# Moving two transposes to other PSUM banks and small steps from VectorE to GpSimd in the first phase of a hybrid attention block

## What is computed

```python
x = x + attn_a(layernorm(x))   # 16 heads of 8: LN, q/k/v, rotary, LN over each head, softmax(q k / sqrt 8) v, output projection
x = x + ffn(layernorm(x))      # r = sigmoid(xr W_r), k = relu(xk W_k)^2, out = r * (k W_v); xr, xk mix a token with the one before
x = x + attn_b(layernorm(x))   # windowed attention, and an MLP updated by one gradient step over all tokens
x = x + ffn(layernorm(x))
```

## Time and profile before

| | us |
|---|---|
| median of 3 runs (1389.87 to 1393.59) | 1391.55 |
| the profiled execution | 1390.66 |
| its span in the trace | 1388.9 |
| first phase: first to last maximum (L783), in the span | 36.0 to 613.9 |
| busy in the stretch 300 to 400: TensorE, VectorE, ScalarE, GpSimd | 96, 90, 85, 64 |

### The profile page before, as it was taken

How to read it: one execution, slowest core, us unless ns; L and a number is a source line. 1 busy time by engine, 2 the same in 40 slices (tenths; PEclk the granted TensorE clock), 3 DMA queues, 4 the chain that set the end, 5 groups by cost and what they waited for, 6 DMA issues and landing times.

```text
span 1388.9 us, 33077 instructions
## 1 busy us (share of the span) xinstructions
PE 1308.6 (94%) x10579; PEld 863.0 (62%) x10579; DVE 1128.7 (81%) x2845; ACT 928.7 (67%) x2570; POOL 507.2 (37%) x815
## 2 busy tenths in 40 slices
PE   6889999999999999987799999999999998999996
PEld 5445555555555555544566666666666665888885
DVE  5788888988999988875788888888888875787876
ACT  3268888888888888875556665665666663556563
POOL 5446666666666666532111111111111100323232
PEclk9899999999999999999999999999999999999998
DMA  2222222223333332210000010000001001223221
GB/s 78 76 75 75 77 77 70 80 79 80 83 90 101 94 78 80 66 42 16 28 28 24 28 57 24 28 28 28 24 28 32 21 17 37 79 84 85 84 85 30
DMA packets 101965, 79.63 MB, mean 57 GB/s; under 512 B 13780, under 2 KB 95124, under 8 KB 101796
## 3 DMA queue, kind: packets, MB, share of 16 engines
q1 hardware_dynamic: 100820, 76.99, 19.9%
q10 hardware_dynamic: 976, 0.54, 0.2%
HBM read 49.70 MB, written 27.79 MB: 56 GB/s over the span
## 4 chain that ended last, share of the span: by engine, by line
PE 49%; DVE 1%; issue 1%; ACT 1%; POOL 0%; POOLq 0%; DVEq 0%; ACTq 0%
PE b_g L1372 4%; PE b_psZ L1388 4%; PE b_psD L1309 4%; PE b_psZ L1320 4%; PE b_g L1359 4%; PE d_psO L1920 4%; PE d_psH L1912 4%; PE b_psR L1365 2%; PE b_psM L1421 2%; PE b_psL L1350 2%; PE b_psR L1381 2%; PE b_psD L1411 2%; PE b_psM L1433 2%; PE d_psG L1938 1%; PE b_psM L1441 1%
## 5 line engine op out<-in xcount | busy, mean ns | idle before, releaser
L783 DVE TENSOR_REDUCE a_MX<-a_psS 128x4 f32<-128x1024 f32 x256 | 312.5, 1221 | 42.9 <-PE a_psS L296 42.7
L586 ACT ACTIVATE a_PT<-a_psE 128x512 f32<-128x512 f32 x504 | 274.3, 603 | 57.5 <-PE a_psE L313 57.2
L1777 POOL TENSOR_TENSOR b_SWB<-b_b2col,b_SW 128x128 f32<-128x128 f32 x65 | 42.9, 660 | 363.5 <-ACT b_SW L1504 363.5
L327 PE MATMUL a_psV<-a_PT,a_VX 128*32 128x256 f32 x2048 | 137.8, 387 | 0.2 <-ACT a_PT L586 0.2
L296 PE MATMUL a_psS<-a_KS,a_QS 48*128 48x256 f16 x1024 | 101.7, 277 | 23.7 <-DVE a_MX L783 19.9
L1522 ACT ACTIVATE b_TH<-b_psZ 128x512 f32<-128x512 f32 x65 | 38.6, 595 | 113.3 <-PE b_psZ L1320 106.3
L313 PE MATMUL a_psE<-a_QS,a_KS 50*128 50x256 bf16 x1008 | 97.5, 270 | 2.4 <-ACT a_PT L586 2.4
L1542 ACT ACTIVATE b_PR<-b_psL,b_mx 128x128 f32<-128x128 f32 x260 | 93.2, 370 | 0.9
L296 PEld LDWEIGHTS a_psS<-a_KS,a_QS 48*128 48x128 bf16 x1024 | 30.1, 94 | 96.2 <-DVE a_MX L783 64.2
L327 PEld LDWEIGHTS a_psV<-a_PT,a_VX 128*32 128x32 f32 x2048 | 53.6, 109 | 51.3 <-issue 28.7
L1663 DVE SCALAR_TENSOR_TENSOR b_HH<-b_TH,b_psZ 128x512 f32<-128x512 f32 x65 | 44.7, 688 | 47.6 <-ACT b_TH L1522 47.6
(11 more groups left out here) (294 smaller groups left out, 3417.0 us busy)
## 6 DMA issues: line engine op xcount, KB each, us to landing
a_KS<-kparts SPq DMA_DIRECT2D x63, 192.0 KB
a_QS<-qparts SPq DMA_DIRECT2D x126, 96.0 KB
qparts<-a_QP SPq DMA_DIRECT2D x64, 96.0 KB, 2.2
a_X<-x_in SPq DMA_DIRECT2D x32, 128.0 KB, 2.4
kparts<-a_KP SPq DMA_DIRECT2D x64, 64.0 KB, 2.1
x<-a_X SPq DMA_DIRECT2D x32, 128.0 KB, 1.8
b_X<-x SPq DMA_DIRECT2D x32, 128.0 KB, 2.2
zT<-b_XT SPq DMA_DIRECT2D x32, 128.0 KB, 1.7
```

Of the source, the lines that this page charges most:

```text
L327: mm = nc.tensor.matmul(psV[32 * h:32 * h + 32, 0:T], VX[:, b % UV, kt, at:at + 32], PT[:, gg, kt, h, :], start=(gg == 0 and kt == 0), sto ...
L586: nc.scalar.activation(PT[:, g % 2, :, h + s, :], shifted_bank(b, p, s), ACT.Exp).then_inc(S["exp"], 1)
L783: nc.vector.reduce_max(MX[:, b % 2, :].rearrange("q (s n) -> q s n", s=2)[:, :, 2 * p:2 * p + 2], psS[:], AX.X).then_inc(S["max"], 1)
```

## The change

Four edits, all in the first phase.

1. The transposed input (`z_t`) goes to the second half of `psC` and not to `psA`, and moves on TensorE from step 4 to step 5, behind `on_t`. `on_t` no longer waits for `zT`; `out_proj` and ScalarE's copy of `on_t` wait instead for z_t's copy and transposes. On ScalarE its copy moves from step 4 to step 5, behind the copy of `on_t` and ahead of `spread`.
2. The transposed maxima (`max_t`) go to `psB` and not to `psC`, and move ahead of `pv(c - 5, 3)` in step 0.
3. The second polynomial step of the inverse root (k = 5 to 7) goes to GpSimd as `rsqrt_end`, four instructions behind `mix`. The temporaries of the steps that stay on VectorE move from PSUM to SBUF tiles (`vr`, `hm`, `hn`).
4. The small affine steps L799, L800 and L869 go to GpSimd, ahead of `power` and of `fpower`.

```diff
@@ tensor
         def max_t(b):
             wait(pe, "max", b, per=NP)
-            wait(pe, "v", b + 3)
-            if b >= B - 3:
-                wait(pe, "x1", b - 3)
-            nc.tensor.transpose(psC[0:32, 0:P], MX[:, b % 2, :], ident[:]).then_inc(S["mxT_ps"], 1)
+            wait(pe, "normed", b + 2)
+            nc.tensor.transpose(psB[0:32, T:T + P], MX[:, b % 2, :], ident[:]).then_inc(S["mxT_ps"], 1)
 
         def zt_bank(b):
-            return psC if b < 3 else psA
+            return psC[:, 0:T] if b < 3 else psC[:, T:2 * T]
@@ z_t
             if b >= 3:
-                wait(pe, "square", b - 1)
-                wait(pe, "centred", b - 1)
+                wait(pe, "on", b - 6)
+                wait(pe, "v", b - 1)
@@ on_t
             wait(pe, "on", b)
-            wait(pe, "zT", b + 6)
             if b < B - 1:
                 wait(pe, "fzT", b - 1, per=4)
@@ tensor body
                 if p == 4:
                     if on(c - 4):
                         pv(c - 4, 1)
-                    if on(c + 1):
-                        z_t(c + 1)
                 if p == 5:
                     if on(c - 5):
                         on_t(c - 5)
+                    if on(c + 1):
+                        z_t(c + 1)
                     if on(c - 6):
                         ffn_kr(c - 6)
@@ scalar body
                 if p == 5:
+                    if on(c - 5):
+                        on_t(c - 5)
+                    if on(c + 1):
+                        z_t(c + 1)
                     if on(c):
                         spread(c)
-                    if on(c - 5):
-                        on_t(c - 5)
@@ vector rsqrt
             if k in (1, 5):
-                nc.vector.tensor_tensor(psyv, hr[:], psvr, ALU.mult).then_inc(S["hrstd"], 1)
+                nc.vector.tensor_tensor(hm[:], hr[:], vr[:], ALU.mult).then_inc(S["hrstd"], 1)
             elif k == 2:
-                nc.vector.tensor_tensor(hn[:], psyv, hr[:], ALU.mult).then_inc(S["hrstd"], 1)
+                nc.vector.tensor_tensor(hn[:], hm[:], hr[:], ALU.mult).then_inc(S["hrstd"], 1)
@@ gpsimd
         def power(b):
+            if b > 2:
+                wait(pool, "stats", b, per=2 * NT)
+                nc.gpsimd.tensor_scalar(s12[:, 0, :], mv[:, :, 1], EPS, None, ALU.add).then_inc(S["affine"], 1)
+                nc.gpsimd.tensor_scalar(s12[:, 1:3, :], mv[:, :, 1].unsqueeze(1).broadcast_to([P, 2, NT]), 1.0 + EPS, EPS * EPS, ALU.mult, ALU.add).then_inc(S["affine"], 1)
             wait(pool, "affine", b, per=2)
@@
+        def rsqrt_end(b):
+            wait(pool, "hrstd", b, per=9, done=5)
+            nc.gpsimd.tensor_tensor(hm[:], hr[:], vr[:], ALU.mult).then_inc(S["hrstd"], 1)
+            wait(pool, "hrstd", b, per=9, done=6)
+            nc.gpsimd.tensor_tensor(hn[:], hm[:], hr[:], ALU.mult).then_inc(S["hrstd"], 1)
+            wait(pool, "hrstd", b, per=9, done=7)
+            nc.gpsimd.tensor_scalar(hn[:], hn[:], -9.0 / 128.0, 1.5, ALU.mult, ALU.add).then_inc(S["hrstd"], 1)
+            wait(pool, "hrstd", b, per=9, done=8)
+            nc.gpsimd.tensor_tensor(hr[:], hn[:], hr[:], ALU.mult).then_inc(S["hrstd"], 1)
@@
         def fpower(b):
+            wait(pool, "fstats", b, per=2 * NT)
+            nc.gpsimd.tensor_scalar(fs[:], fmv[:, :, 1], EPS, None, ALU.add).then_inc(S["faffine"], 1)
             wait(pool, "faffine", b)
@@ gpsimd body
             if on(c):
+                rsqrt_end(c)
                 x_bias(c)
```

More of the change, by code:

```diff
@@ L396, in var @@
             wait(pe, "normed", b - 1)
+            wait(pe, "mT", b - 3)
             for t in range(NT):
@@ L403, in hr_t @@
             wait(pe, "spread", b)
-            wait(pe, "hrstd", b, per=8)
+            wait(pe, "hrstd", b, per=9)
             for t in range(NT):
@@ L411, in out_t @@
             wait(pe, "ot", b, per=2)
-            wait(pe, "mT", b + 2)
             if b >= B - 2:
@@ L431, in out_proj @@
             wait(pe, "onT", b)
-            wait(pe, "onT", b)
+            if b < B - 6:
+                wait(pe, "zT", b + 6)
             for t in range(NT):
@@ L454, in ffn_kr @@
             wait(pe, "centred", b + 6)
-            wait(pe, "zT", b + 7)
             if b >= B - 6:
@@ L481, in body @@
                         proj_q(c)
+                    if on(c - 3):
+                        max_t(c - 3)
                     if on(c - 5):
                         pv(c - 5, 3)
-                    if on(c - 3):
-                        max_t(c - 3)
                 if p == 1:
@@ L603, in z_t @@
             wait(act, "q_ps", b - 1)
-            nc.scalar.activation(ZT1[:], (psC if b < 3 else psA)[:, 0:T], ACT.Copy).then_inc(S["zT"], 1)
+            nc.scalar.activation(ZT1[:], psC[:, 0:T] if b < 3 else psC[:, T:2 * T], ACT.Copy).then_inc(S["zT"], 1)
         def proj_v(b):
@@ L630, in spread @@
         def spread(b):
-            wait(act, "hrstd", b, per=8)
+            wait(act, "hrstd", b, per=9)
             wait(act, "hrT_ps", b - 1)
@@ L647, in on_t @@
             wait(act, "onT_ps", b)
+            if b < B - 6:
+                wait(act, "zT_ps", b + 6)
             wait(act, "outp_ps", b - 1)
@@ L818, in variance @@
             wait(dve, "erad", b)
-            wait(dve, "hrstd", b - 1, per=8)
-            nc.vector.tensor_tensor(psvr.rearrange("q (t n) -> q t n", t=NT), psB[:, 0:64].rearrange("q (t n) -> q t n", t=NT),
+            wait(dve, "hrstd", b - 1, per=9)
+            nc.vector.tensor_tensor(vr[:].rearrange("q (t n) -> q t n", t=NT), psB[:, 0:64].rearrange("q (t n) -> q t n", t=NT),
                                     erad[:].unsqueeze(2).broadcast_to([P, NT, 32]), ALU.add).then_inc(S["vareps"], 1)
@@ L826, in rsqrt @@
                 wait(dve, "spread", b - 1)
[L827 removed]
+                nc.vector.tensor_scalar(hr[:].bitcast(I32), vr[:].bitcast(I32), -0.5, float(0x5f3759df), ALU.mult, ALU.add).then_inc(S["hrstd"], 1)
                 return
[L829 removed]
+            wait(dve, "hrstd", b, per=9, done=k)
             if k in (1, 5):
[L831 removed]
+                nc.vector.tensor_tensor(hm[:], hr[:], vr[:], ALU.mult).then_inc(S["hrstd"], 1)
             elif k == 2:
[L833 removed]
+                nc.vector.tensor_tensor(hn[:], hm[:], hr[:], ALU.mult).then_inc(S["hrstd"], 1)
             elif k == 3:
[L835 removed]
+                nc.vector.scalar_tensor_tensor(out=hm[:], in0=hn[:], scalar=-10.0 / 3.0, in1=hn[:], op0=ALU.add, op1=ALU.mult).then_inc(S["hrstd"], 1)
             elif k == 4:
[L837 removed]
+                nc.vector.scalar_tensor_tensor(out=hr[:], in0=hm[:], scalar=5.0, in1=hr[:], op0=ALU.add, op1=ALU.mult).then_inc(S["hrstd"], 1)
             elif k == 6:
[L839 removed]
+                nc.vector.scalar_tensor_tensor(out=hn[:], in0=hm[:], scalar=-9.0 / 128.0, in1=hr[:], op0=ALU.mult, op1=ALU.mult).then_inc(S["hrstd"], 1)
             elif k == 7:
[L841 removed]
+                nc.vector.scalar_tensor_tensor(out=hr[:], in0=hn[:], scalar=1.5, in1=hr[:], op0=ALU.add, op1=ALU.mult).then_inc(S["hrstd"], 2)
         def normed(b):
@@ L947, in body @@
                         rsqrt(c, 4)
-                        rsqrt(c, 5)
                 if p == 6:
@@ L1293, in tensor @@
         pe.wait_ge(A["normed"], B)
+        pe.wait_ge(A["mT"], B)
         nc.tensor.matmul(psM[:], fold[:], w1_t[:], start=True, stop=False)
```

20 lines of the change are left out of this document (3 added, 17 removed).

## The result

The changed kernel takes 1407.74 us in the median of four runs (1405.42 to 1409.29) against 1390.71 for the kernel before in the same runs (1389.31 to 1393.59): a ratio of 1.0116, 95% interval 1.0097 to 1.0135. It is slower, near the 1406 forecast. The profiled executions span 1404.7 and 1388.9, so 15.8 us are to be found.

A forecast was written before the change was run, and what follows sets the result against it. Waits between TensorE and VectorE were taken to bound the first phase. `on_t` 0.22, `z_t` 0.25 and KA 0.10 made 0.57 us a round, over 26 rounds 14.8, so 1391.55 became 1406 us; range 1399 to 1413, chance 0.50.

The forecast's parts named there:

- What bounds the kernel: First phase: waits between TensorE and VectorE decide; step 4 at its 1.80 us floor, step 5 TensorE's, steps 6 and 7 on TensorE.
- The path: Steps 3 to 5: FZ 0.5 us late without slack, so ScalarE's copies are late and the FP copy releases `on_t`.
- Affine steps: GpSimd ahead of `power` and `fpower`: three small instructions make FZ ready 0.54 us later, taken as 0.5 (0.3 to 0.65).
- There is none: Slack between FZ's end (318.79) and its transposes on TensorE (318.92): claimed to be none.
- `on_t` 0.22 later: Step 5 on TensorE: the late FP copy ends at 322.41, so `on_t` starts at 322.51, 0.22 us later.
- `z_t` 0.25: Step 5 on TensorE: the moved transposes add 0.25 us between `on_t` and `ffn_kr`, delaying step 6's scores.
- `spread` and KA, 0.1: After GpSimd's `rsqrt_end`: `spread` later on ScalarE, then GpSimd's KA, delaying `ffn_v`; taken as 0.1 us a round (0 to 0.4).
- `max_t` 0: Step 0 on TensorE: `max_t` only changes places with `pv`, so it costs 0.
- Sum: 0.22 + 0.25 + 0.10 = 0.57 us a round, over 26 rounds 14.8 us; rounds at both ends put at 0.
- Rival 1: Step 3: VectorE's k = 0 to 2, held by GpSimd up to 0.45 us each, decide; likeliest 1420 us, chance 0.22.
- Rivals 2 and 3: Rival 2: faster, FZ not late, 1386 to 1387 us, chance 0.14; rival 3: no change, FZ's delay absorbed, 1393, chance 0.14.
- What would show it: Trace signs: aggregates to FZ's transposes 4.3 us, not 3.8; FP copy releases `on_t`; VectorE's idle before step 6's maximum grows 0.5.

The follow-up runs named there:

- e3: The changed kernel with the three small affine steps back on VectorE and its root temporaries back in PSUM: 1386.84 us, ratio 0.9959.
- e4: The kernel before with edits 1 and 2 alone (bank and place of `z_t` and `max_t`): 1385.25 us, ratio 0.9952.
- e2: The changed kernel with VectorE's root temporaries back in PSUM and one added copy of the variance to SBUF for GpSimd: 1407.96 us, ratio 1.0113.
- e11: The kernel before with edits 1, 2 and 4, the whole root on VectorE in PSUM: 1407.52 us, ratio 1.0097.
- e8: The kernel before with only `on_t`'s wait for `zT` left out: 1390.31 us, ratio 0.9985.
- e9: The kernel before with edits 1 and 2, but `max_t` back behind `pv` in step 0: 1387.61 us, ratio 0.9953.
- e10: The kernel before with edits 1 and 2 and the root's temporaries in SBUF, root and affine steps on VectorE: 1398.29 us, ratio 1.0036.

## Why the prediction was right, and where it was not

**What bounds the kernel** held. Step 5 was TensorE's, removing k = 5 to 7 gave nothing (e3 equals e4), and steps 6 and 7 passed everything through: 2.58 and 1.96 in all fourteen kernels.

**The path** held as drawn: FZ late, the copies late, `on_t` released by the FP copy (0.14 behind its end in 21 of 24 rounds). The prediction had named its own refutation, "if TensorE, not the copies, released `on_t`"; the list of waits looks like it, and the starts say that it did not happen.

**Affine steps: the place right, the size too small.** "FZ is ready 0.54 later; ... I take 0.5": its end measured 0.78 later (4.45 behind the aggregates instead of 3.67), its transposes 0.71. Two hand-overs were missed. The two instructions before `power` have one between them and one behind them; 320.47 ends at 320.67 and `power` starts at 320.75, so it starts 0.68 after the aggregates instead of 0.35: 0.33, not 0.24. For `fpower` 0.30 was taken; from `power`'s start to L1078's it is now 1.72. The kernel before needed 1.29 there, as its L1070 starts 0.03 ahead of `power`'s end (315.47 + 1.32):

```profile
316.76 0.70 POOL L1070 TENSOR_TENSOR a_fs<-a_fs,a_mhalf 128x2 f32<-128x2 f32 x1
```

So a 0.21 instruction cost 0.43: it brings its own hand-over and ends the overlap of its neighbours. My guess that overlap would make the sum smaller pointed the wrong way.

**"There is none", of the slack behind FZ,** was right within 0.07, but the first to feel it was overlooked. The prediction followed the copies to `on_t`. The transposes themselves stand in TensorE's queue ahead of step 4's scores, and those are late by the same 0.66 two steps earlier. In e2 and e11 that delay is given back in part (step 4 at its floor, 1.84 to 1.85), and the FP copy decides there too, in 23 and 22 rounds.

**`on_t` 0.22 later:** counted from the aggregates' end, 7.17 before, now 327.74 - 320.07 = 7.67: 0.50 later. 0.21 of the difference is FZ's; most of the rest is that `on_t` starts 0.14 behind the copy where 0.10 was taken, so that its slack was 0.23 and not 0.28 (e8).

**`z_t` 0.25:** 0.16 in e4's and 0.15 in the changed kernel's step 5 (327.74 to 329.17 is 1.43, before 1.28). The sum took no gain for the vanished wait, rightly: 0.21 in e4, used up by the late FP copy here. Later by 0.50 + 0.15 = 0.65 at step 6's scores, where 0.47 was forecast.

**`spread` and KA, 0.1:** the waits came as predicted (ScalarE for GpSimd's root 21 times, the fv matmuls for KA 23 times), and cost nothing: steps 6 and 7 did not change. `max_t` 0: it gains 0.05 (e4 against e9).

**Sum.** 0.57 a round forecast, 0.58 measured by the median. That it fits so well is luck: `on_t` was put 0.28 too low, and `z_t`, KA and `max_t` together 0.25 too high (0.50 + 0.15 - 0.05 = 0.60). Over the 26 rounds 14.8 were forecast and 16.2 measured; two falls of the clock, 0.9 us each, for which the sum had no term, are part of the rest. The rounds at both ends, put at 0, made -0.3.

**Rivals.** Rival 1's price was real: k = 1 took 0.885 us in the changed kernel, and in e10, where nothing covers the holds, a round is 0.45 longer. Its point from which it decides was step 4's maximum starting 0.53 late. It started 0.69 late (325.73 - 320.07 = 5.66, before 320.09 - 315.12 = 4.97) and did not decide: the FP copy was later than forecast too, `on_t` can follow the scores after 0.54 and not 0.62, and most of the 0.69 came with the scores, which moved with FZ. The e2 run confirms it. A detail was wrong: "No VectorE instruction of the full rounds does that before". k = 3 (L835 of before) names `hn` twice, both SBUF, with GpSimd idle beside it; in e11 it is held, 384 ns on average where e3 has 224. Even e2's temporaries in PSUM leave this one held (376). Rivals 2 and 3 needed FZ not late; e4 (1385.25) shows rival 2's place, without edit 4.

**By "What would show it"** a reader would have found: 4.51 instead of 4.3; the FP copy as what releases `on_t`, though by the starts and not by the list; no gap between `on_t`, `z_t` and `ffn_kr`; ScalarE waiting for GpSimd ahead of `spread`; KA; and, for rival 1, k = 1 held. VectorE's idle time ahead of step 6's maximum grew from 0.59 to 0.94, not by 0.5.

The Trainium skill ("SBUF — State Buffer", Who interferes with whom) says that a VectorE instruction with two SBUF inputs contends with a GpSimd instruction that reads SBUF. The trace agrees with that: k = 1 took 885 ns beside GpSimd, 229 with one input in PSUM. The table of the Trainium skill ("VectorE: DVE Perf Modes", the TRN2 errata) charges a fixed 58 cycles for an SBUF source and 120 for a PSUM source. The rows show no such difference: with 64 columns, e3's k = 2 from PSUM took 224 ns and the changed kernel's k = 4 from SBUF alone, unheld, 225 (L835).

## What to carry to other kernels

Before moving a small instruction to an engine that looks idle, ask who stands behind it in that engine's stream and what stands behind those customers in *their* queues; price it as its row plus one hand-over (about 0.1), plus the overlap that it breaks. Where two paths end at one wait, undo both, each and neither: here one undone alone gave nearly everything and the other nothing. To find which of two arrivals decides, look for the one whose distance to the waiting instruction stays the same from round to round and kernel to kernel; a list of waits leaves out the short ones. Compare the median round beside the mean, and the granted clock beside both. An order that frees one product of an in-order engine delays the next, so look at the whole stretch between two of its idle times.
